# Reordering the last attention body: both halves' first scores together, three transposed score products behind them, and the last shift rows turned in another PSUM bank

## The reference

```
x = x + tanh(g_xattn[0]) * depool_and_project(layernorm(x), ctx)     # stage A
x = x + tanh(g_ffn[0])   * coupled_cycles(layernorm(x))              # stage B, 3 cycles
x = x + tanh(g_xattn[1]) * cross_attention(ctx, layernorm(x), mask)  # stage C
x = x + tanh(g_ffn[1])   * low_rank_ffn(layernorm(x))                # stage D
```

```
# C: 8 heads of 32 channels, 256 x 256 scores for each sequence and head
scores = q @ k.T / sqrt(32); scores[masked] = -inf
out = concat(x_n, softmax(scores) @ v) @ W_out.T + b_out
# D: rank 64, 1024 hidden
out = gelu(x_n @ U1 @ V1 + b1) @ U2 @ V2 + b2
```

## Time and profile before

| what | value |
|---|---|
| median of three runs | 698.32 us |
| profiled execution, its own time | 698.65 us |
| span of its trace | 696.5 us |
| PE (matmul) busy | 658.6 us, 95% |
| ACT busy | 451.7 us, 65% |
| DVE busy | 427.9 us, 61% |
| POOL busy | 201.9 us, 29% |

### The profile page before, as it was taken

One profiled execution on the slowest core, in us unless ns is written; L12 is line 12 of the kernel. 1 busy time (PEld: TensorE's weight loads), 2 busy tenths in 40 slices (PEclk: granted clock), 3 DMA queues, 4 the chain that ended last, 5 costly groups with the idle time before them and its releaser, 6 DMA issues.

```text
span 696.5 us, 11909 instructions
## 1 busy us (share of the span) xinstructions
PE 658.6 (95%) x3653; PEld 457.5 (66%) x3653; DVE 427.9 (61%) x981; ACT 451.7 (65%) x1204; POOL 201.9 (29%) x299
## 2 busy tenths in 40 slices
PE   5799899999999999799999999999999998799997
PEld 3565555555544457688888887888888875556654
DVE  7854757776775647566767576566665685343522
ACT  7656655535545543667887787778778877646452
POOL 6565423310110003224432342333223230142110
PEclk9999999999999999999999999999999999999999
DMA  8731116601000005434344443433444331001112
GB/s 280 224 106 61 51 41 233 106 1 61 1 0 1 0 1 123 93 95 101 93 115 123 124 104 88 116 95 93 117 122 121 92 69 25 2 1 61 43 50 90
DMA packets 45809, 57.90 MB, mean 83 GB/s; under 512 B 13152, under 2 KB 24258, under 8 KB 45634
## 3 DMA queue, kind: packets, MB, share of 16 engines
q1 hardware_dynamic: 45762, 57.33, 30.5%
HBM read 27.46 MB, written 4.19 MB: 45 GB/s over the span
## 4 chain that ended last, share of the span: by engine, by line
PE 82%; SPq 5%; ACT 3%; DVE 3%; issue 2%; POOL 2%; DMA 2%; DVEq 0%; POOLq 0%; ACTq 0%
PE bank L1191 12%; PE bank L1493 7%; PE bank L1405 7%; PE bank L1423 6%; PE bank L1203 6%; PE bank L1446 5%; PE bank L1469 4%; PE bank L1636 4%; PE bank L1486 4%; SPq L531 4%; PE bank L1432 4%; PE bank L1167 3%; PE bank L1626 3%; PE bank L1171 2%; PE bank L1627 2%
## 5 line engine op out<-in xcount | busy, mean ns | idle before, releaser
L970 ACT ACTIVATE c_junk<-bank,c_nmx 128x256 bf16<-128x256 f32 x256 | 116.3, 469 | 9.3 <-DVE c_nmx L1961 9.2
L1961 DVE TENSOR_REDUCE c_nmx<-bank 128x4 f32<-128x1024 f32 x64 | 75.3, 1219 | 34.8 <-PE bank L1446 34.8
L1191 PE MATMUL bank<-b_o,cw 128*128 128x512 f32 x192 | 90.8, 603 | 0.2 <-ACT b_o L827 0.2
L803 ACT ACTIVATE b_h<-bank,cb 128x512 f32<-128x512 f32 x48 | 32.8, 686 | 51.2 <-PE bank L1191 51.2
L1090 ACT ACTIVATE d_h<-bank,b_col 128x512 f32<-128x512 f32 x64 | 39.6, 686 | 39.4 <-PE bank L1627 39.4
L992 ACT ACTIVATE c_pT<-bank 128x1024 f32<-128x1024 f32 x64 | 62.0, 1017 | 4.8 <-PE bank L1469 3.7
L1405 PE MATMUL bank<-c_ctxT,wsrcT 128*128 128x256 f32 x256 | 61.8, 386 | 0.0
L1191 PEld LDWEIGHTS bank<-b_o,cw 128*128 128x128 f32 x192 | 34.2, 190 | 41.3 <-issue 39.2
L1423 PE MATMUL bank<-wsrcT,c_ctxT 128*128 128x256 f32 x240 | 56.7, 379 | 0.0
L1469 PE MATMUL bank<-c_stack 99*128 99x256 f32 x256 | 46.7, 315 | 6.6 <-DMA c_stack<-c_rows 6.4
L1405 PEld LDWEIGHTS bank<-c_ctxT,wsrcT 128*128 128x128 f32 x256 | 48.3, 193 | 6.3
(11 more groups left out here) (202 smaller groups left out, 1384.2 us busy)
## 6 DMA issues: line engine op xcount, KB each, us to landing
c_stack<-c_parts SPq DMA_DIRECT2D x192, 128.0 KB
a_ctx<-in_ctx SPq DMA_DIRECT2D x16, 512.0 KB, 4.0
c_ctx<-in_ctx SPq DMA_DIRECT2D x16, 512.0 KB, 3.3
out_x<-x_sb SPq DMA_DIRECT2D x7, 512.0 KB, 2.9
x_sb<-in_x SPq DMA_DIRECT2D x3, 1024.0 KB, 10.2
mask_b<-in_mask_BxS_fk SPq DMA_DIRECT2D x1, 2048.0 KB, 12.8
x_sb<-in_x SPq DMA_DIRECT2D x2, 512.0 KB, 5.5
wsrc_raw<-in_L_xattn_W_src SPq DMA_DIRECT2D x1, 1024.0 KB, 7.3
```

The lines of the kernel that those rows point to most:

```text
L970: op = nc.scalar.activation(c_junk[:, tc, j, :], scores(tc)[:, j, :], ACT.Exp, bias=c_nmx[hg][:, tc, j:j + 1], accum_out=c_sum[hg][:, tc, ...
L1191: op = mm(bank[2 * u + h][:], cw1[:, c, h * P:(h + 1) * P], b_o[n % LANES][:, c, :], start=c == 0, stop=c == DK - 1)
L1961: v.tensor_reduce(c_nmx[hg][:, tc, :], scores(tc), AXIS.X, ALU.max, negate=True)\
```

## The change

The order on PE, ACT and DVE is rewritten in `last_c` alone. The first scores of (15, 1) come directly behind the turn of the shift rows of (15, 0). The two transposed products of (14, 1) and the first one of (15, 0) follow. The turn of the last shift rows goes to bank 5. The waits are set to match: which product frees which banks is another one now. The two transposed products of (15, 1) move from behind the body into it.

```diff
+def rows_bank(b, hg):
+    return 5 if is_last(b, B) and hg == 1 else 6
...
@@ ACT, last_c
-                probsT_c(b - 1, 1, 0)
-                probsT_c(b - 1, 1, 1)
                 rows_c(b, 0)
-                update_c(b - 1, 1 - s, 1)
                 sums_c(b, 1, 0)
                 sums_c(b, 1, 1)
                 logs_c(b, 1)
+                probsT_c(b - 1, 1, 0)
+                probsT_c(b - 1, 1, 1)
+                rows_c(b, 1)
                 probsT_c(b, 0, 0)
+                update_c(b - 1, 1 - s, 1)
                 probsT_c(b, 0, 1)
-                rows_c(b, 1)
                 update_c(b, s, 0)
...
@@ PE, scores_c and scoresT_c
-                    need(pe, c_pT_ok, TS * (n - 2) + tc + 1)
+                    if is_last(b, B) and hg == 1:
+                        pe.wait_ge(c_sum_ok, TS * (n - 1) + tc + 1)
+                    else:
+                        need(pe, c_pT_ok, TS * (n - 2) + tc + 1)
...
-                need(pe, c_rows_in, 16 * TS * (n + 1))
-                if is_last(b, B) and hg == 1:
-                    need(pe, c_pT_ok, TS * n + q + 1 - TS)
+                need(pe, c_rows_in, 16 * TS * (n + (2 if is_at(b, B - 2) and hg == 1 else 1)))
+                if is_last(b, B):
+                    pe.wait_ge(c_pT_ok, TS * n + q + 1 - TS)
+                elif is_at(b, B - 2) and hg == 1:
+                    pe.wait_ge(c_sum_ok, TS * (n + 2) + q + 1)
...
@@ PE, update_c
-                if is_last(b, B) and hg == 0:
-                    pe.wait_ge(c_rows_ok, 2 * B)
...
@@ PE, last_c
-                out_begin(b - 1, 1 - s, 0)
-                scoresT_c(b - 1, 1 - s, 1, 0)
+                out_begin(b - 1, 1 - s)
                 lowrank_d(1)
-                scoresT_c(b - 1, 1 - s, 1, 1)
                 rows_c(b, 0)
                 scores_c(b, s, 1)
+                scoresT_c(b - 1, 1 - s, 1, 0)
+                scoresT_c(b - 1, 1 - s, 1, 1)
+                scoresT_c(b, s, 0, 0)
+                rows_c(b, 1)
                 update_c(b - 1, 1 - s, 1)
+                scoresT_c(b, s, 0, 1)
                 out_c(b - 1, 1 - s)
-                scoresT_c(b, s, 0, 0)
-                out_begin(b, s, 0)
-                scoresT_c(b, s, 0, 1)
-                rows_c(b, 1)
+                scoresT_c(b, s, 1, 0)
                 update_c(b, s, 0)
+                scoresT_c(b, s, 1, 1)
+                out_begin(b, s)
...
@@ DVE, last_c
                 maxima_c(b, s, 1)
+                lowrank_d(1)
+                shift_c(b, 1)
                 finish_c(b - 1, 1 - s)
-                shift_c(b, 1)
-                lowrank_d(1)
```

More of the change, by code:

```diff
@@ L985, in rows_c @@
                 need(act, c_rows_in, 16 * TS * (n - 1))
-                nc.scalar.copy(c_rows[hg][:], bank[6][0:TS * SHIFTS * QH, hg * S:hg * S + P]).then_inc(c_rows_ok, 1)
+                nc.scalar.copy(c_rows[hg][:], bank[rows_bank(b, hg)][0:TS * SHIFTS * QH, hg * S:hg * S + P]).then_inc(c_rows_ok, 1)
             def probsT_c(b, hg, q):
@@ L1454, in rows_c @@
                     pe.wait_ge(b_x2, NG)
-                need(pe, c_up_ok, n - 1 if is_last(b, B) else n)
+                if is_last(b, B) and hg == 1:
+                    pe.wait_ge(d_xT_ok, 2 * LEAD - 1)
+                else:
+                    need(pe, c_up_ok, n - 1 if is_last(b, B) else n)
                 nc.tensor.transpose(
-                    bank[6][0:TS * SHIFTS * QH, hg * S:hg * S + P],
+                    bank[rows_bank(b, hg)][0:TS * SHIFTS * QH, hg * S:hg * S + P],
                     c_shift[hg][:].rearrange("p k a j -> p (k a j)").bitcast(F32), ident[:]).then_inc(c_rows_ps, 1)
@@ L1516, in xnT_d @@
                     pe.wait_ge(c_q_ok, B)
+                    if n == LEAD:
+                        pe.wait_ge(c_rows_ok, 2 * B)
                     need(pe, d_xT_ok, 2 * n - 1)
@@ L1618, in _ @@
             over_batches(pe, body_c)
-            scoresT_c(B - 1, 1, 1, 0)
-            scoresT_c(B - 1, 1, 1, 1)
             def hidden_d(n, j):
```

## The result

The changed kernel took 701.60 us (median of 13 runs, 700.76 to 704.34), the kernel before 698.38 us (13 runs beside them). The ratio is 1.0045, with a 95% interval from 1.0031 to 1.0059: 3.2 us slower, by little, but clear of the noise. A second comparison later gave 1.0049 (1.0030 to 1.0067).

What follows compares the result with a forecast made beforehand. The last body was taken as bound by a chain round the engines; 1.03 gained at the rows' copy, lost again plus 1.53, gave +1.5 us: 700.2 from 698.65, less 0.33 for the median, 699.8; range 698.0 to 701.5.

Steps and rivals of the forecast that it cites:

- rival 2: Last body: two half-rate stretches on end, slowing sequence 14's output product too; +2.5 to +4.2, 700.8 to 702.5; chance 0.09.
- rival 4: Stage D, behind the last body: the delay is absorbed there, giving 698.3; chance 0.08.
- The clock: PE's clock in the last body: emptier PE might bring half rate, by the skill's rule; counted only in rivals.
- rival 1: Last body: one half-rate stretch, beginning before 592, to 595 at most; up to +1.0, total +1.5 to +2.5; chance 0.32.
- PE loses its filling here: Before the turn of the rows of (15, 0): two transposed products gone, only the low-rank product (1.08 us) left.
- The order's term: Last body: 1.03 gained at the copy of the rows, lost again and 1.53 more behind it; sum +1.5 us.
- Then the queues decide: ACT, last body: copy of the update of (15, 0) stands ahead of the last exponentials, 599.39 instead of 597.86, loss 1.53.
- The sums 0.64 earlier: ACT, last body: sums of (15, 1) begin at 587.24 instead of 587.88, no update copy ahead of them.
- The gain of 1.03 at the copy of the rows: ACT, last body: the last shift rows are copied at 593.34 instead of 594.37.
- PE's idle time in the stretch: PE, last body: a sign of being right would be more idle time by about 1.5 us.
- The low-rank copies on DVE hidden: DVE, before the shift of (15, 1): two pairs of 0.85 us hidden behind the sums; uncovered, up to 1.7.
- The turn in bank 5 at no cost: PE, last shift rows: same matmul as at 593.78, costs nothing; its wait for a stage D copy is long met.

Runs made afterwards that it cites:

- the filled kernel: The changed kernel with 13 extra matmuls that no one reads in PE's gaps of the last body: 699.86 us, 1.0002 of the kernel before.
- the second trace: The changed kernel unaltered, run and profiled again beside the kernel before: 702.11 us, ratio 1.0049.
- The two matmuls more: Two extra matmuls ahead of the transposed products of (15, 1), in the filled kernel (700.08 us, 1.0002) and in the kernel before (698.65 us, 0.9984).
- the two versions with the shorter stretch: The kernel before with last rows turned in bank 5 and three moves (698.76 us, 0.9999); that version with three more moves on ACT and PE (697.12 us, 0.9967).
- the thinned kernel: The kernel before with 6 of 8 matmuls left out of the two transposed products of (14, 1): 702.63 us, 1.0049.

## Why the prediction was wrong

The direction was in it, and the measured 701.6 lies 0.1 us above the range of 698.0 to 701.5. The forecast of 699.8 was 1.8 us too low. The ends of the range were also not what I called them: the middle of rival 2 (700.8 to 702.5) is 701.65, and rival 4 less 0.1 is 698.2.

**The step that failed is "The clock".** I put this term at 0 in the forecast and at "up to +1.0" for one stretch of half rate, as rival 1, with 0.32. It measured 1.5 us in the profiled run and 2.5 in the second. Three things were wrong in it. I looked for the empty stretch between 586.5 and 592.4. The first fall came before that, at 585.3, behind the gap of 580.4 to 584.9, which the two moved products had helped to fill. I had written "PE loses its filling here" of exactly that gap and priced only its idle time, at nothing. Then I took the length of the half rate from one place in one execution; here it lasted 10.2 us and more. The gap of 586 to 592 lay inside it, and with that gap filled it lasted 3.4; but the place of the earlier trace rows itself had 10.2 us in the trace of the changed kernel, so one reading was no bound. And I held the gaps of the last body of before against it, though the new ones are much emptier: 1.08 of 4.30 us busy against 2.49. Counted from the start of the stretch against the filled kernel, the changed one is 0.18 us late at the first transposed product of (14, 1), behind the slow first scores, 0.69 at the update, behind a slow product and turn, and 1.49 behind the slow update. So the delay was paid where rival 1 had put it, at more than its "up to +1.0". Rival 2, with 0.09, was right that the half rate would go on, and its 700.8 to 702.5 holds the result; but the output product that it made slow ran at its full rate (1.13 at 596.30), so its size fits by luck. In the second trace that product was touched (1.36). The Trainium skill's page "TensorE: Matmul & The Clock Gate", section "HAM oscillation — how this bites in real kernels", warned that idle gaps bring the throttle back. The traces agree (0.50 from 585.4 to 595.6 and from 585.0 to 597.4), though these gaps were not wholly idle. I had named that rule in the prediction and given it no time in the forecast.

**The order's term was right in size.** I summed +1.53; with the clock full the stretch has +1.75. In the filled kernel, counted from the start of the stretch and set on 577.59, the copy of the rows is at 593.41 (I had 593.34), the update at 593.37 (593.35), the output product at 594.95 (594.91), the first transposed product of (15, 1) at 597.44 (597.42), the last exponentials at 599.61 (599.39), the last output product at 604.33 (604.11). The 0.2 left comes from one size: behind the output product, four matmuls of fp32r (one record each) hold PE for 0.76 (596.82 - 596.06), not 0.57. In the changed kernel it is 0.76 there too (599.56 - 598.80).

**Its reason was half wrong.** "Then the queues decide", I wrote, and meant the copy on ACT ahead of the last exponentials. With the copy behind them the exponentials came 1.3 earlier and the stretch gained 0.19. The reason that the traces give is that PE is full from 591 on: the work that it did under the sums before (update and output product of sequence 14) now stands in one row with all that follows. The two matmuls more show it. That the sum came out right was luck in part: both queues had the same length to within 0.2.

**Other steps.** The sums 0.64 earlier: with a full clock they are at 587.25, set on 577.59, against my 587.24. The gain of 1.03 at the copy of the rows: 1.0 with a full clock, and 0.4 (594.01) in the changed kernel, 0.2 when set on the same start, where the product and the turn before it ran at half rate. PE's idle time in the stretch rose by 0.8, from 6.42 (24.99 - 18.57) to 7.23 (28.25 - 21.02), and not by 1.5: work at half rate counts as busy for longer. The low-rank copies on DVE hidden: yes, DVE waited for the logs behind them. The turn in bank 5 at no cost: not tried alone; it is part of the two versions with the shorter stretch. Rival 4, absorption in stage D: none, 86.06 of 88.20.

## What to carry to other kernels

Where an engine waits, ask what it did in the wait: work moved out of it costs up to its own length again if the engine is full behind, and nothing if it is not; two extra matmuls at the place in question tell which. On PE a filled wait can also keep the clock: compare the busy time of each gap before and after, not only the idle time on the path. Take an emptied gap as a warning and not as a threshold, since gaps with the same work in them went both ways here, and price the half rate by what lies behind it. And when the rows or sums are the path, move them ahead in the queues one by one and leave the filling under them.

## What the runs showed of the hardware that I had not expected

A half rate can last while PE is nearly full: 6.2 us with 5.71 busy in the thinned kernel, most of it at 0.50. Its length differs between executions of the same code: 3.4 and 10.2 us at the place of the earlier trace rows, 10.2 and 13.6 in the last body of the changed kernel. What it cost here, by one trace each, went with what lay under it: 0.47 us where it lay over the fillers (27.21 - 26.74), 2.16 where it lay over the full part (28.90 - 26.74), and nothing that the start of the stretch shows at the early place. Taking 6 of 3653 matmul records out made the kernel 0.5% slower (1.0049). Putting 13 matmuls into the changed kernel brought its ratio to before from 1.0045 to 1.0002.
